# Cross-attention and expert layer on one core: order of the first two pairs' query tiles, one rotation moved to GpSimd, and the banks of two weight products

## The chip, the core and the metric

One core of a Trainium2 chip runs the kernel. The metric is the device time of one execution in microseconds (us). The program writes its own instruction streams, one for each engine: TensorE (PE), VectorE (DVE), ScalarE (ACT), GpSimd (POOL) and SyncE (SP, which only starts DMAs). An engine takes its instructions in the order written, and semaphores make it wait for another's.

## What is computed

The reference, cut to what matters. `x` is 2 x 256 rows of 256, `ctx` 2 x 512 rows of 64; there are 16 heads and 32 experts.

```
h = layernorm(x)
q = rope((h @ Wq.T per head) @ w_kc_q)          # 192 per head
scores = (q @ W_qr) @ (rope(ctx) @ W_kr).T      # 256 x 512 per head and batch
x = x + (softmax(scores) @ rope(ctx) @ w_kc_kv.T per head) @ Wo.T
h = layernorm(x)
top 4 of 32 experts by sigmoid(h @ gate.T) + bias, in 2 of 4 groups
x = x + sum of the chosen experts' swiglu(h) * weight + shared swiglu(h)
```

## The kernel before

**Tiling.** The 16 heads are worked in four groups of four, each group as two pairs. The attention consists of 64 score tiles (128 queries x 512 keys of one head and batch), numbered t. Pair 0 has tiles 0 to 7, pair 1 tiles 8 to 15, and so on. Three banks of PSUM (2, 3, 4) hold scores, two (5, 6) the transposed probabilities, bank 7 the attended sums, and banks 0 and 1 (`shared`) all that is prepared for later pairs. The change touches only the first 41 us of the program.

**Steps.** What is prepared is written as steps `(group, letter, index)`:

- `M0` to `M3`: the product of one head's two query weights (PE, L505); ACT casts it to the high part (L851, L852), DVE subtracts for the low part (L1054, semaphore `m_lo`).
- `A`, `B`, `C` with index j: the three 128-row tiles of pair j's queries, six matmuls each (L456 to L458). Tile A holds rows of the pair's first head, B of its second, C the rest of both.
- Rotation of such a tile. By GpSimd: ACT copies the tile out of its bank (L867) and half of it shifted (L868), DVE copies the other half shifted (L1061: the exchange, semaphore `q_swap`), then GpSimd does three operations (L361, L362, L364). By DVE straight from the bank (L1044 twice, L1046, L1047), when the tile stands in `AHEAD`; steps `x` and `z` name the place of the rotation of tiles A and C. The first B tile (`ALONE`) goes to GpSimd with all three copies by ACT (L864, L865, L868).
- `G`: product of the two rotation-side weights, into `gmat` (PE L511, ACT L856). `R0 R1 R2` (pair 0) and `P0 P1 P2` (pair 1): the rotated tiles A, B, C times `gmat`, added up in one bank (L537, L537, L540); then ACT casts (L875, L876) and DVE subtracts (L1080, L1082, semaphore `q_lo`), and the pair's scores can start.
- `N`: product of two output-side weights (PE L516, ACT L858). `K`: transposes of the keys (L554) with their high part (ACT L887) and low part (DVE L1093, semaphore `kT_lo`). `X`: transposes of the normalised rows. `W`: filler matmuls. `E`: a table load.

**A score tile.** PE computes it (L583, L584), DVE takes the row maximum (L1097), ACT the exponential with its sum (L893), PE transposes the probabilities (L595), ACT (t even) or DVE (t odd) copies them to `pT` (L902, L1115), and PE multiplies by the rows of ctx (L612, `attend`).

**What sets the order.** `PROLOGUE` is the list of steps ahead of the first score; `PLAN[g]` says which steps stand at which tile of group g. A step with "-" belongs to the group itself, one without it to the next group: `M0` in `PLAN[0]` is the second group's. `SEQ` joins them, and each engine walks the same list for its own share. `USED` are the steps of `SEQ` that take a bank. Those in `OWN_BANK` have a fixed one; the rest (`SHARED`) alternate between banks 0 and 1 in the order of the list, so that step n waits until step n-2 has left the bank: for an `M` that is `m_lo` of its subtraction, for `R` or `P` it is `q_lo`, for a tile in `AHEAD` its rotation, for anything else the copy out of the bank. An `R` or `P` counts at the place of its index 2, though its index 0 is the first to write. Scores of t wait for the exponential of t-3.

**Names of the change's place.** `first_turned` is the special form of the first query tile, `bank_free` the waits for a bank, `scores(0)` and `transposes(0)` the first of each. In the loop of PE `steps(0)` stands between scores 2 and scores 3; on ACT and DVE between the exponentials and maxima of tiles 2 and 3 and the work of tile 0's probabilities.

## Time and profile before

| | |
|---|---|
| median of 3 runs | 302.06 us (301.9 to 302.15) |
| the profiled execution | 301.82 us, of which the span of the profile is 299.5 us |
| TensorE busy | 282.5 us (94%), mean granted clock 0.995 |
| VectorE, ScalarE, GpSimd busy | 181.4, 156.4, 129.5 us |
| HBM | 30.38 MB read, 3.67 MB written |

Times of rows are us from the span's start. A timeline row gives the start, the time from the start of its first to the end of its last instruction, the engine, the line, the operation and its tiles, and in brackets the idle time before it with what ended that. Matmuls overlap: one of 512 columns in the fast format lasts 0.40 us in its row while the next starts 0.23 us after it. A plain f32 matmul has two records.

### The profile page before, as it was taken

To read this page: it belongs to the slowest core of one execution; us is meant where nothing else is said; L and a number is where in the kernel's file an instruction comes from. 1 tells how busy PE (TensorE), PEld (TensorE's weight loads), DVE (VectorE), ACT (ScalarE), POOL (GpSimd) and SP (SyncE) were. 2 spreads that over 40 slices of the span, in tenths; PEclk is the share of its full clock that TensorE was granted. 3 is DMA by queue.
4 is the path that set the end of the run, shared out by engine and by line. 5 is a ranking of instruction groups with operands and counts; after the bars stand their busy time and mean duration, and the time that the engine had idled before them with its cause. 6 is when DMAs were issued, how large, how long until landed. Compare 5 with 4: busy or idle time off the path is not lost.

```text
span 299.5 us, 5458 instructions
## 1 busy us (share of the span) xinstructions
PE 282.5 (94%) x1831; PEld 202.7 (68%) x1831; DVE 181.4 (61%) x434; ACT 156.4 (52%) x373; POOL 129.5 (43%) x121
## 2 busy tenths in 40 slices
PE   8988799999999999999999999978789999999982
PEld 6857568676777666787667777754567666676662
DVE  4877776576757777765854466158842233344676
ACT  2747469675785866777773355185212333343330
POOL 0656328791036770079940000000176555565572
PEclk9999999999999999999999999999999999999998
DMA  7962500001700001600039992402033544432234
GB/s 235 402 253 79 204 1 2 0 2 25 255 3 1 0 3 46 218 0 1 2 127 380 402 352 78 173 2 70 1 106 106 150 150 144 154 109 72 70 82 130
DMA packets 15994, 34.41 MB, mean 115 GB/s; under 512 B 2528, under 2 KB 8416, under 8 KB 15968
## 3 DMA queue, kind: packets, MB, share of 16 engines
q1 hardware_dynamic: 13664, 27.77, 26.0%
q0 software_dynamic: 2304, 6.29, 7.4%
q8 instruction: 16, 0.26, 0.4%
q14 instruction: 10, 0.08, 0.1%
HBM read 30.38 MB, written 3.67 MB: 114 GB/s over the span
## 4 chain that ended last, share of the span: by engine, by line
PE 85%; DVE 7%; DMA 2%; issue 2%; ACT 2%; POOL 1%; POOLq 0%; DVEq 0%; ACTq 0%
PE bank L719 10%; PE bank L612 10%; PE bank L595 9%; PE bank L583 5%; PE bank L562 5%; PE bank L584 4%; PE bank L740 4%; PE bank L456 4%; PE bank L458 4%; PE bank L457 4%; PE bank L505 3%; PE bank L708 3%; PE bank L537 3%; PE bank L685 3%; PE bank L540 3%; PE bank L463 2%
## 5 line engine op out<-in xcount | busy, mean ns | idle before, releaser
L1413 POOL DMA_INDIRECT rope<-xn_rows,idx x32 | 31.2, 974 | 83.3 <-DVE idx L1307 61.9
L893 ACT ACTIVATE prob<-bank,nmax 128x512 f32<-128x512 f32 x48 | 32.7, 685 | 38.9 <-DVE nmax L1097 38.9
L361 POOL TENSOR_TENSOR rtmp<-abuf,rope 128x512 f32<-128x512 f32 x20 | 25.7, 1284 | 60.4 <-PE bank L458 41.0
L1097 DVE TENSOR_REDUCE nmax<-bank 128x1 f32<-128x512 f32 x64 | 41.2, 685 | 8.7 <-PE bank L584 8.4
L719 PE MATMUL bank<-wall,nmat 128*64 (+1 forms) x256 | 31.2, 386 | 0.8 <-ACT nmat L968 0.8
L612 PE MATMUL bank<-pT,kvr 128*64 128x256 f32 x256 | 31.2, 386 | 0.0
L1115 DVE COPY pT<-bank 128x512 f32<-128x512 f32 x32 | 22.0, 687 | 13.1 <-PE bank L595 12.9
L583 PE MATMUL bank<-kdup,qsp 128*128 128x512 f32 x64 | 28.3, 442 | 1.2 <-ACT prob L893 1.2
L364 POOL TENSOR_TENSOR roped<-rtmp 128x512 f32<-128x512 f32 x20 | 25.9, 1295 | 1.6
L1314 DVE TENSOR_TENSOR kv<-bank,kv 128x256 f32<-128x256 f32 x16 | 6.8, 425 | 32.5 <-ACT kv L981 32.4
L595 PE MATMUL bank<-ident,prob 128*128 128x128 f32 x192 | 26.3, 273 | 0.0
L595 PEld LDWEIGHTS bank<-ident,prob 128*128 128x128 f32 x192 | 22.6, 141 | 4.9 <-issue 1.7
L362 POOL TENSOR_TENSOR rtmp<-abuf,rope 128x512 f32<-128x512 f32 x20 | 25.8, 1292 | 0.0
L584 PE MATMUL bank<-kdup,qsp 128*128 128x512 f32 x64 | 25.3, 395 | 0.0
L719 PEld LDWEIGHTS bank<-wall,nmat 128*64 128x64 f32 x256 | 16.9, 137 | 10.5 <-issue 3.5
L612 PEld LDWEIGHTS bank<-pT,kvr 128*64 128x64 f32 x256 | 16.9, 137 | 9.8 <-issue 2.8
L902 ACT COPY pT<-bank 128x512 f32<-128x512 f32 x32 | 18.9, 592 | 7.5 <-PE bank L595 7.2
L1061 DVE COPY abuf<-bank 64x512 f32<-64x512 f32 x20 | 13.7, 684 | 14.7 <-ACT abuf L867 14.4
L968 ACT COPY nmat<-bank 128x512 f32<-128x512 f32 x16 | 9.4, 585 | 23.3 <-PE bank L708 23.3
L1418 POOL DMA_INDIRECT ctT<-y_rows,place x16 | 16.3, 1017 | 10.3 <-PE bank L719 3.7
L456 PE MATMUL bank<-xnT,msplit 128*128 128x512 f32 x46 | 20.6, 447 | 0.0
L583 PEld LDWEIGHTS bank<-kdup,qsp 128*128 128x128 f32 x64 | 12.0, 188 | 9.2 <-issue 7.4
(217 smaller groups left out, 559.8 us busy)
## 6 DMA issues: line engine op xcount, KB each, us to landing
wall<-in_w_exp SPq DMA_DIRECT2D x32, 384.0 KB, 7.5
wring<-in_w_attn SPq DMA_DIRECT2D x16, 224.0 KB, 4.3
wring<-in_w_attn SPq DMA_DIRECT2D x4, 640.0 KB, 8.1
y_rows<-nmat SPq DMA_DIRECT2D x10, 256.0 KB, 2.1
wring<-in_w_attn SPq DMA_DIRECT2D x4, 512.0 KB, 7.0
rope<-in_rope_q SPq DMA_DIRECT2D x1, 768.0 KB, 7.0
x_sb<-in_x SPq DMA_DIRECT2D x1, 512.0 KB, 3.6
xn_rows<-xn SPq DMA_DIRECT2D x4, 128.0 KB, 1.7
```

Source lines behind the costliest of these rows:

```text
L361: eng.tensor_tensor(t0.rearrange("p (b s) -> p b s", b=B), own.rearrange("p (b s) -> p b s", b=B), cos, ALU.mult)
L362: link(eng.tensor_tensor(t1.rearrange("p (b s) -> p b s", b=B), other.rearrange("p (b s) -> p b s", b=B), sin, ALU.mult))
L364: return eng.tensor_tensor(roped[:, j, k, :], t0, t1, ALU.add)
L456: pe.matmul(out_ap, a_hi, b_hi, start=first, stop=False)
L583: pe.matmul(s_ps[t % 3][:, :], q, kdup[:, 0, b * L:(b + 1) * L], start=True, stop=False)
L584: pe.matmul(s_ps[t % 3][:, :], q, kdup[:, 1, b * L:(b + 1) * L], start=False, stop=True) \
L595: mm = pe.transpose(t_ps[t % 2][:, lc * P:(lc + 1) * P], probs[t % 4][:, lc * P:(lc + 1) * P], ident[:, :])
L612: mm = pe.matmul(pv_ps[hh * DC:(hh + 1) * DC, 0:S], kvr[:, b * LC + lc, 0, :], pT[:, (2 * n + hh) % PR, lc, :], start=(lc == 0), stop=(lc ...
L719: mm = pe.matmul(hu_ps[j % 2][s * BLK:(s + 1) * BLK, (u % 2) * 2 * I:(u % 2 + 1) * 2 * I], xTu[:, u % XS, dc, s * BLK:(s + 1) * BLK], wall ...
L893: act.activation(probs[t % 4], s_ps[t % 3][:, :], ACT.Exp, bias=nmax[:, t:t + 1], accum_out=psum_e[:, t:t + 1]).then_inc(s_exp, 1)
L1097: dve.tensor_reduce(nmax[:, t:t + 1], s_ps[t % 3][:, :], AX.X, ALU.max, negate=True).then_inc(s_max, 1)
L1413: pool.indirect_dma_start(xg[:, u % XG, :], None, xn_dram, bass.IndirectOffsetOnAxis(idx[:, u:u + 1], 0)) \
```

## The change

Six edits. (1) In `PROLOGUE` B of pair 0 comes ahead of A and takes the form `first_turned`; A follows. (2) The two N products get banks 2 and 3 and other places: N0 behind R0, N1 behind R2. (3) The last step of the prologue, B of pair 1, becomes `FIRST`; PE does it where it did, but ACT takes its copies behind the exponentials of tiles 0 and 1, and DVE its exchange behind their maxima. (4) C of pair 1 leaves `AHEAD`: its rotation goes from DVE to GpSimd, with two copies by ACT and an exchange by DVE. (5) On PE only G of pair 1 stays between scores 2 and 3; C of pair 1 stands behind scores 3. (6) At tile 4 the order is P0, P1, A0, P2 in place of P0, P1, P2, A0; A0 is the second group's first query tile.

```diff
--- before.py
+++ after.py
@@ -287,7 +287,7 @@
 
 
         PLAN = [
-            {0: "-G1", 1: "-C1 -z1", 2: "M0", 3: "M1", 4: "-P0 -P1 -P2 A0", 6: "B0", 7: "C0 G0", 8: "M2 M3", 9: "A1 G1", 10: "B1 R0 R1 R2", 11: "C1", 13: "N0", 15: "P0 P1 P2"},
+            {0: "-G1 -C1", 2: "M0", 3: "M1", 4: "-P0 -P1 A0 -P2", 6: "B0", 7: "C0 G0", 8: "M2 M3", 9: "A1 G1", 10: "B1 R0 R1 R2", 11: "C1", 13: "N0", 15: "P0 P1 P2"},
             {0: "-N1", 3: "M0 M1", 6: "A0 B0 M2", 7: "G0 M3 C0", 9: "z0 A1 B1", 10: "R0 R1 R2", 11: "C1", 12: "G1", 14: "P0 P1", 15: "P2 N0"},
             {1: "-N1", 2: "M0", 3: "M1", 6: "A0 B0", 7: "M2 C0", 8: "G0 M3", 10: "A1 B1", 11: "R0 R1 R2 C1", 13: "N0", 14: "G1", 15: "N1"},
             {0: "-P0 -P1 -P2", 2: "O0 O1 O2 O3", 8: "O4", 11: "S0", 15: "O5 O6"},
@@ -299,18 +299,19 @@
             for s in PLAN[g].get(t % TPG, "").split():
                 yield (g, s[1], int(s[2])) if s[0] == "-" else (g + 1, s[0], int(s[1]))
 
-        PROLOGUE = [(0, s[0], int(s[1])) for s in "W6 M0 M1 W1 X0 M2 E0 W1 A0 x0 B0 C0 z0 M3 G0 K0 N0 R0 N1 R1 R2 A1 B1".split()]
-
-        SEQ = PROLOGUE + [s for t in range(TILES) for s in steps(t)]
+        PROLOGUE = [(0, s[0], int(s[1])) for s in "W6 M0 M1 W1 X0 M2 E0 W1 B0 A0 x0 C0 z0 M3 G0 K0 R0 N0 R1 R2 N1 A1".split()]
+        FIRST = (0, "B", 1)
+
+        SEQ = PROLOGUE + [FIRST] + [s for t in range(TILES) for s in steps(t)]
         USED = [s for s in SEQ if s[1] in "MGABCN" or (s[1] in "RP" and s[2] == NQT - 1)]
         USE = {s: u for u, s in enumerate(USED)}
         BY_DVE = [(NPG * g + i, "xyz".index(kind)) for g, kind, i in SEQ if kind in "xyz"]
         BY_POOL = [(p, k) for p in range(NP) for k in range(NQT) if (p, k) not in BY_DVE]
 
-        AHEAD = ((0, "A", 0), (0, "C", 0), (0, "C", 1))
+        AHEAD = ((0, "A", 0), (0, "C", 0))
         ALONE = (0, "B", 0)
         TURNED = [s for s in USED if s[1] in "ABC" and s not in AHEAD and s != ALONE]
-        OWN_BANK = {(0, "M", 2): 2, (0, "M", 3): 3, (0, "C", 0): 4, (0, "B", 1): 5}
+        OWN_BANK = {(0, "M", 2): 2, (0, "M", 3): 3, (0, "C", 0): 4, (0, "N", 0): 2, (0, "N", 1): 3, (0, "B", 1): 5}
         SHARED = [s for s in USED if s not in OWN_BANK]
 
         def work(u):
@@ -464,7 +465,7 @@
 
             def first_turned(u):
 
-                m_hi, m_low = m_v[:, 0, :, 0, 0, :], m_v[:, 1, :, 0, 0, :]
+                m_hi, m_low = m_v[:, 0, :, 0, 1, :], m_v[:, 1, :, 0, 1, :]
                 pe.wait_ge(wk_out, out_count(use(0, "M", 1)))
                 for dc in range(ND):
                     pe.wait_ge(xT_hi, dc + 1)
@@ -480,8 +481,10 @@
             def bank_free(u):
 
                 n = SHARED.index(USED[u]) if USED[u] in SHARED else 0
-                if USED[u] == (0, "B", 1):
+                if USED[u] == FIRST:
                     pe.wait_ge(kT_lo, 2)
+                elif USED[u][:2] == (0, "N"):
+                    pe.wait_ge(m_lo, OWN_BANK[USED[u]] + 1)
                 if n >= 2:
                     g, kind, i = SHARED[n - 2]
                     if kind == "M":
@@ -518,7 +521,7 @@
                     mm.then_inc(wk_full, 1)
                 elif kind in "ABC":
                     k = "ABC".index(kind)
-                    if u == use(0, "A", 0):
+                    if u == use(0, "B", 0):
                         first_turned(u)
                         return
                     pe.wait_ge(m_lo, HG * g + 2 * i + 2)
@@ -577,6 +580,7 @@
                 if t == 0:
                     pe.wait_ge(kT_lo, 2)
                     pe.wait_ge(m_lo, HG)
+                    pe.wait_ge(wk_out, out_count(use(0, "N", 1)))
                 if t >= 3:
                     pe.wait_ge(s_exp, t - 2)
                 q = qsp[:, p % QR, hh, b * S + st * P:b * S + (st + 1) * P]
@@ -587,8 +591,8 @@
             def transposes(t):
                 pe.wait_ge(s_exp, t + 1)
                 if t == 0:
-                    pe.wait_ge(wk_out, out_count(use(0, "B", 1)))
-                    pe.wait_ge(q_swap, TURNED.index((0, "B", 1)) + 1)
+                    pe.wait_ge(wk_out, out_count(use(*FIRST)))
+                    pe.wait_ge(q_swap, TURNED.index(FIRST) + 1)
                 if t >= 2:
                     await_out(pe, t - 2)
                 for lc in range(LC):
@@ -618,23 +622,23 @@
             for s in PROLOGUE:
                 step(*s)
             pe.wait_ge(kT_lo, 2)
+            step(*FIRST)
             for t in range(LOOK):
                 scores(t)
+            between, *behind = steps(0)
             for t in range(TILES):
                 if t % 2 == 0:
                     for u in range(t + LOOK, min(t + LOOK + 2, TILES)):
                         if u == LOOK + 1:
-                            for s in steps(0):
-                                step(*s)
+                            step(*between)
                         scores(u)
                 n, late = divmod(t - ALAG, 4)
                 if late == 0 and n >= 0:
                     attend(n)
                 if late == 1 and n >= 0:
                     quotients(n)
-                if t >= 1:
-                    for s in steps(t):
-                        step(*s)
+                for s in steps(t) if t else behind:
+                    step(*s)
                 if t % 2 == 0:
                     transposes(t)
                     transposes(t + 1)
@@ -912,6 +916,7 @@
                 step(*s)
             for t in range(LOOK):
                 exps(t)
+            step(*FIRST)
             for t in range(TILES):
                 if t % 2 == 0:
                     for u in range(t + LOOK, min(t + LOOK + 2, TILES)):
@@ -1125,6 +1130,7 @@
                 step(*s)
             for t in range(LOOK):
                 row_max(t)
+            step(*FIRST)
             for t in range(TILES):
                 if t % 2 == 0:
                     for u in range(t + LOOK, min(t + LOOK + 2, TILES)):
```

Where the instructions stand, at three places. First PE in the prologue, around the three matmuls of R (`roped,gmat`) and the two of each N (`wring 64x256`), before:

```order
L516 MATMUL bank1<-wring 64x256 [waits d_wn0,wk_out]
L516 MATMUL bank1<-wring 64x256
L537 MATMUL bank1<-roped,gmat 64x512 [waits rope_a,wk_out]
L516 MATMUL bank0<-wring 64x256 [waits d_wn0,wk_out]
L516 MATMUL bank0<-wring 64x256
L537 MATMUL bank1<-roped,gmat 64x512 [waits rope_p]
L540 MATMUL bank1<-roped,gmat 128x512 [waits rope_a]
L456 MATMUL bank0<-xnT,msplit 128x512 [waits m_lo,wk_out]
```

and now:

```order
L540 MATMUL bank1<-roped,gmat 64x512 [waits rope_a,wk_out]
L519 MATMUL bank2<-wring 64x256 [waits d_wn0,m_lo]
L519 MATMUL bank2<-wring 64x256
L540 MATMUL bank1<-roped,gmat 64x512 [waits rope_p]
L543 MATMUL bank1<-roped,gmat 128x512 [waits rope_a]
L519 MATMUL bank3<-wring 64x256 [waits d_wn0,m_lo]
L519 MATMUL bank3<-wring 64x256
L457 MATMUL bank0<-xnT,msplit 128x512 [waits m_lo,wk_out]
```

R0 no longer stands behind N0 in the same bank, and N1 has moved behind R2. Second DVE, from the exchange of B of pair 1 (`abuf<-bank5`) to the second group's first two subtractions (`msplit`), before:

```order
L1061 COPY abuf<-bank5 64x512 [waits q_own]
L1097 TENSOR_REDUCE nmax<-bank2 128x1 [waits s_mm]
L1097 TENSOR_REDUCE nmax<-bank3 128x1 [waits s_mm]
L1097 TENSOR_REDUCE nmax<-bank4 128x1 [waits s_mm]
L1097 TENSOR_REDUCE nmax<-bank2 128x1 [waits s_mm]
L1115 COPY pT<-bank6 128x4x128 [waits t_mm]
L1044 TENSOR_TENSOR rtmp<-bank0,pT 64x512 [waits wk_full,d_turn]
L1044 TENSOR_TENSOR rtmp<-bank0,pT 64x512
L1046 TENSOR_TENSOR rtmp<-bank0,rope 128x512 [waits d_rope]
L1047 TENSOR_TENSOR roped<-rtmp 128x512 [waits chain_v]
L1097 TENSOR_REDUCE nmax<-bank3 128x1 [waits s_mm,rope_a]
```

and now:

```order
L1102 TENSOR_REDUCE nmax<-bank3 128x1 [waits s_mm]
L1066 COPY abuf<-bank5 64x512 [waits q_own]
L1102 TENSOR_REDUCE nmax<-bank4 128x1 [waits s_mm]
L1102 TENSOR_REDUCE nmax<-bank2 128x1 [waits s_mm]
L1066 COPY abuf<-bank0 64x512 [waits q_own]
L1120 COPY pT<-bank6 128x4x128 [waits t_mm]
L1102 TENSOR_REDUCE nmax<-bank3 128x1 [waits s_mm]
L1102 TENSOR_REDUCE nmax<-bank4 128x1 [waits s_mm]
```

The exchange of B (`bank5`) stands behind the second maximum and ahead of the third; an exchange for C (`bank0`) stands where no instruction of C stood, and the four of its rotation are gone. Third PE at tile 4, P0 and P1 (`64x512`), P2 and the second group's A0, before:

```order
L537 MATMUL bank1<-roped,gmat 64x512 [waits rope_p,wk_out,m_lo]
L537 MATMUL bank1<-roped,gmat 64x512 [waits rope_p]
L540 MATMUL bank1<-roped,gmat 128x512 [waits rope_a]
L456 MATMUL bank0<-xnT,msplit 128x512 [waits m_lo]
```

and now:

```order
L540 MATMUL bank0<-roped,gmat 64x512 [waits rope_p,wk_out,m_lo]
L540 MATMUL bank0<-roped,gmat 64x512 [waits rope_p]
L457 MATMUL bank1<-xnT,msplit 128x512 [waits m_lo]
...
L543 MATMUL bank0<-roped,gmat 128x512 [waits rope_p]
```

P0, P1 and P2 now write bank 0, which the second group's M1 used last, in place of bank 1, which its M0 used last; P2 stands behind the six matmuls of A0 and waits for GpSimd in place of DVE.

## Rows read from the trace of the kernel before

**Rows 1.** The page's busy times.

```profile
PE 282.5 (94%) x1831; PEld 202.7 (68%) x1831; DVE 181.4 (61%) x434; ACT 156.4 (52%) x373; POOL 129.5 (43%) x121
```

**Rows 2.** Waits of PE up to 66 us: us in total, times, longest.

```profile
PE bank L505 <- DVE roped L1047: 0.5, 1, 0.5
```

**Rows 3.** Windows: length, then busy us of PE, PEld, DVE, ACT, POOL, clock, DMA.

```profile
211.00:214.00 3.00, 1.33 (x18) 1.21 (x18) 2.42 (x11) 1.43 (x4) 0.00 (x0) 1.00 0.00 0
```

**Rows 4.** Timeline of PE, the prologue.

```profile
18.55 0.64 PE L537 MATMUL bank<-roped,gmat 128*64 128x512 f32 x1 [0.86 <-ACT nmat L858]
...
19.65 0.64 PE L537 MATMUL bank<-roped,gmat 128*64 128x512 f32 x1
```

**Rows 5.** The chain that ended last, in order of time: start, us.

```profile
20.72 1.06 PE bank L540 x2
```

**Rows 6.** Timeline of DVE, the prologue.

```profile
12.17 1.39 DVE L1044 TENSOR_TENSOR rtmp<-bank,pT 64x512 f32<-64x512 f32 x2 [0.23 <-PE bank L477]
...
15.28 1.39 DVE L1044 TENSOR_TENSOR rtmp<-bank,pT 64x512 f32<-64x512 f32 x2
...
18.50 0.62 DVE L1054 TENSOR_TENSOR msplit<-bank,msplit 128x256 fp32r<-128x256 f32 x2
```

**Rows 7.** Timeline of ACT, the prologue.

```profile
13.49 0.59 ACT L864 COPY abuf<-bank 128x512 f32<-128x512 f32 x1 [0.95 <-PE bank L458]
```

**Rows 8.** Timeline of POOL, 14 to 29 us.

```profile
14.09 0.61 POOL L1390 COPY kvr<-kvr 128x512 f32<-128x512 f32 x1
15.41 1.27 POOL L361 TENSOR_TENSOR rtmp<-abuf,rope 128x512 f32<-128x512 f32 x1 [0.71 <-ACT abuf L868]
...
18.00 1.60 POOL L364 TENSOR_TENSOR roped<-rtmp 128x512 f32<-128x512 f32 x1
24.70 1.30 POOL L361 TENSOR_TENSOR rtmp<-abuf,rope 128x512 f32<-128x512 f32 x1 [5.11 <-DVE abuf L1061]
...
27.30 1.28 POOL L364 TENSOR_TENSOR roped<-rtmp 128x512 f32<-128x512 f32 x1
28.67 1.29 POOL L361 TENSOR_TENSOR rtmp<-abuf,rope 128x512 f32<-128x512 f32 x1
```

**Rows 9.** Timeline of DVE, 25 to 38 us.

```profile
25.23 0.68 DVE L1061 COPY abuf<-bank 64x512 f32<-64x512 f32 x1 [0.70 <-ACT abuf L867]
25.95 1.89 DVE L1097 TENSOR_REDUCE nmax<-bank 128x1 f32<-128x512 f32 x3
...
30.68 1.39 DVE L1044 TENSOR_TENSOR rtmp<-bank,pT 64x512 f32<-64x512 f32 x2 [0.77 <-PE bank L458]
...
33.53 1.29 DVE L1097 TENSOR_REDUCE nmax<-bank 128x1 f32<-128x512 f32 x2
36.16 0.62 DVE L1054 TENSOR_TENSOR msplit<-bank,msplit 128x256 fp32r<-128x256 f32 x2 [1.34 <-ACT msplit L852]
...
37.30 0.61 DVE L1054 TENSOR_TENSOR msplit<-bank,msplit 128x256 fp32r<-128x256 f32 x2
```

**Rows 10.** Timeline of ACT, 26 to 36 us.

```profile
26.67 0.69 ACT L893 ACTIVATE prob<-bank,nmax 128x512 f32<-128x512 f32 x1 [0.87 <-DVE nmax L1097]
...
27.35 0.68 ACT L893 ACTIVATE prob<-bank,nmax 128x512 f32<-128x512 f32 x1
...
29.74 0.47 ACT L856 COPY gmat<-bank 128x384 f32<-128x384 f32 x1
30.10 0.60 ACT L902 COPY pT<-bank 128x512 f32<-128x512 f32 x1
34.25 0.69 ACT L893 ACTIVATE prob<-bank,nmax 128x512 f32<-128x512 f32 x1 [3.56 <-DVE nmax L1097]
```

**Rows 11.** Timeline of PE, 24 to 37 us.

```profile
24.65 0.40 PE L584 MATMUL bank<-kdup,qsp 128*128 128x512 f32 x1
...
27.59 0.48 PE L583 MATMUL bank<-kdup,qsp 128*128 128x512 f32 x1 [0.95 <-ACT prob L893]
...
36.84 1.08 PE L537 MATMUL bank<-roped,gmat 128*64 128x512 f32 x4 [0.95 <-DVE msplit L1054]
```

## The prediction

> **What bounds the kernel now.** The page comes first: PE is busy 94% of the span, every other engine 61% or less [rows 1]. So PE's own work sets the time wherever PE has no wait, and an edit that removes no PE work can only win by shortening PE's waits. The list of PE's waits, cut to the first 66 us, then says which there are, and the timeline of PE where each stands. Four of some size lie where this change can touch them. At 18.55, R0 waits 0.86 us for ACT's copy of N0 [rows 4]. At 27.59, scores 3 wait 0.95 for the second exponential [rows 11]. M1 of the second group waits 0.5 for DVE's rotation of C of pair 1 [rows 2].  At 36.84, P0 waits 0.95 for the subtraction of the second group's M0 [rows 11]. From there to the output products of the last group PE has no wait in that list. So the whole effect of this change is read from one point: how much earlier or later P0 starts than 36.84. Behind it the same matmuls follow in nearly the same order.
>
> **The prologue.** B of pair 0 is now the first product. DVE took up the first product at 12.17 [rows 6], ACT took up the second at 13.49, behind an idle time of 0.95, so it had been free from 12.54 [rows 7]. Now ACT starts its three copies at 12.55, 0.94 earlier. GpSimd's rotation began at 15.41 [rows 8]; it cannot win all of it, because GpSimd's own copy of the ctx rows (L1390) ends at 14.70 [rows 8], so I start it at 14.79, 0.62 earlier. It took 4.19, to 19.60 [rows 8], so it ends at 18.98 and R1 starts at 19.03 in place of 19.65 [rows 4]. DVE's rotation of A moves the other way: 1.32 later, from 12.17 to 13.49. It takes 3.11 (12.17 to 15.28) and the one of C 3.22 (15.28 to 18.50) [rows 6], so C is rotated at 19.82. R1 to R2 took 1.07 (19.65 to 20.72), R2 took 1.06 [rows 4, 5]. Now R2 starts at 20.10, so C is in time by 0.28, and ends at 21.16. R0's wait of 0.86 is gone, but it was no gain: with R0 at 17.04, PE waits for GpSimd in R1 all the same. N1 stood inside the wait and now stands behind R2, where it costs PE 0.43 to 0.58; I take 0.49. So A of pair 1 starts at 21.65 in place of 21.78: **a gain of 0.13**.
>
> Here two engines meet. DVE's two rotations took 3.11 and 3.22 beside GpSimd's work [rows 6], while the one of C of pair 1, with GpSimd idle at its end, took 2.85 (30.68 to 33.53) [rows 9]; and GpSimd's L364 took 1.60 at 18.00 against 1.28 at 27.30 [rows 8]. What meets is the last of DVE's four operations (L1047), the one that reads SBUF alone. The two of these now fall at about 15.6 and 18.7, other places of GpSimd's rotation; I leave the stretch as it was, one on each engine. The Trainium skill (SBUF — State Buffer, Terms) has it that the two engines lock one port pair for a whole instruction and that the loser fully blocks. The trace shows stretches of a third of a microsecond, less than a whole 1.28 us instruction. By that rule GpSimd could end about 0.5 us later, and the sum would come out near 302.9.
>
> **The maxima ahead of the exchange.** DVE's first maximum began at 25.95 because the exchange of B of pair 1 (25.23) stood ahead of it [rows 9]. Its scores were ready at 25.05 (24.65 + 0.40 [rows 11]), 25.08 at DVE. With the 0.13 it now starts at 24.95, 1.00 earlier; the first exponential, 0.72 behind it, goes from 26.67 [rows 10] to 25.67, and scores 3 from 27.59 [rows 11] to 26.59. That is the change's gain, and if nothing came back it would be 1.00 us at PE.
>
> **What comes back.** The B copy now stands on ACT behind the second exponential and the exchange on DVE behind the second maximum, with the third and fourth maxima queued behind it. Exponentials follow each other by 0.68 or 0.66, so the copy starts at 27.01 (0.59 long), the exchange at 27.64, and the third maximum at 28.35, while in the old order it stood at 27.2, the third of three from 25.95 [rows 9]. The fourth starts 0.63 later and the fourth exponential at 29.75 in place of 29.06 (0.68 ahead of 29.74 [rows 10]). Then ACT copies G (to 30.43, and 0.36 until the next, as 29.74 to 30.10), copies C (30.79), DVE exchanges C (31.42), copies the probabilities of tile 1 (32.13) and takes the fifth maximum at 32.84. Before it was 33.53, behind the 2.85 us of C's rotation. So of the 2.85 taken from DVE only 0.69 remains, since ACT reaches C's copy so late. The fifth exponential goes from 34.25 [rows 10] to 33.56. On PE in that time: C (six matmuls, 1.40) runs at 27.05, hidden; the transposes of tile 2 now wait for the copy of tile 0's probabilities, which ACT makes behind C's two copies (31.97 to 32.55, formerly 30.10), and run at 32.6; M1 and scores 6 and 7 are done at 35.1. PE then waits for P0.
>
> **The bank.** P0 started 2.59 behind the fifth exponential (34.25 to 36.84), 0.06 behind the end of M0's subtraction (36.16 + 0.62). In the new order of the list A0 counts ahead of P2, so P0 to P2 take bank 0, whose last user is M1, and P0 waits for M1's subtraction. That one stands behind the copy of tile 3's probabilities and ended at 37.91 (37.30 + 0.61) [rows 9], 3.66 behind the fifth exponential. So P0 starts at 33.56 + 3.66 + 0.06 = 37.28 in place of 36.84. **A loss of 0.44.** C's rotation on GpSimd covers itself: A's starts at about 24.6, one takes 3.97 (24.70 to 28.67 [rows 8]), B's runs from 28.6 to 32.5 and C's to 36.5; P2 at 39.7 is in time. Three GpSimd operations and two ACT copies (1.2 us) thus cost nothing further. P2 behind A0 delays pair 1's `q_lo` by what A0 takes, 1.40; by the same walk it is there 0.3 before scores 8 want it, since they move by 0.44 too.
>
> **The sum.** -0.13 (N and GpSimd) - 0.87 (exchange) + 0.31 (what comes back until the fifth exponential: 1.00 less 0.69) + 1.13 (bank: 3.72 for 2.59) = +0.44 us. The profiled execution took 301.82, so it would take 302.26; the median of the runs is 302.06, 0.24 above it, so the median goes to **302.5 us**, no change by the bound of 0.2% (0.60 us), which is about what a measurement can tell.
>
> **Rivals.**
>
> Slower: the first rotations are late. Start point: R1, if GpSimd's rotation ends after about 19.3. DVE's two additions each meet a GpSimd instruction; if GpSimd is stretched twice by the 0.32 seen once, and N1 costs its full 0.58, A of pair 1 starts near 22.1, 0.3 later than before, and all behind it shifts: 0.44 + 0.45 = +0.89, 302.95. For it: 1.60 against 1.28. Against it: of the three rotations that GpSimd made up to 33 us only one was stretched, and DVE's additions are short. It decides nothing as long as R1 starts before 19.2. The rule above is this mechanism at its strongest. Chance 0.20.
>
> Faster: the turn of the bank costs nothing. If P0 goes at M0's subtraction, or the pair of subtractions comes closer together, the 0.69 at the fifth exponential reaches PE: 36.15, and 301.4. For it: that is the gain the chain above carries up to 33.56. Against it: the written order and `bank_free` give P0 the wait for M1. Chance 0.12; with it go errors of the same sign, every link of the chain from 24.95 to 37.28 being a little shorter than taken.
>
> Nothing moves: the parts cancel to within 0.2 us, because ACT's copy of C comes earlier than I think or the slack of GpSimd and DVE, both ahead after this, removes small waits later. 302.1. Chance 0.11.
>
> The clock: PE would be idle from 35.1 to 37.3, longer than any wait of before. In the window from 211 to 214 us PE was busy 1.33 of 3 us, with one wait of 1.7, and the granted clock stayed 1.00, that is 2.4 GHz [rows 3]. If the clock fell to 1.2 GHz behind the new wait, the 3.4 us of matmuls up to the transposes of tile 4 would take twice as long: 305.9. The Trainium skill (TensorE: Matmul & The Clock Gate, What's actually happening) says that an idle array is throttled to 1.2 GHz; no row here shows a fall. Chance 0.02.
>
> **How the numbers follow.** My forecast has 0.55, with a range of its own from 302.2 to 302.8 (each of the some nineteen links is good to 0.02, the start of A of pair 1 to 0.2). With the four rivals that makes 1.00. The range from 301.4 to 303.1 takes in the slower case and the nearer half of the faster one, and leaves out some 0.15. Faster by over 0.2% (below 301.46): the faster rival and a rest, 0.13. Slower by over 0.2% (above 302.66): 0.19 of the late rotations' 0.20, the clock's 0.02 and a share of 0.05 of the forecast's own, 0.26. Within: 0.61.
>
> **What would show it.** After the change: R1 at 19.0, A of pair 1 at 21.65, first maximum at 24.95, scores 3 at 26.6; the third maximum not before 28.3, with the wait put down to the exchange or ACT's copy; the fifth exponential at 33.5; then PE's longest wait up to 66 us, some 2.2 us, ahead of P0 and behind the subtraction of M1. It is wrong if P0 starts before 36.8, if PE has a new wait at the transposes of tile 0 or at scores 8, or if the granted clock leaves 1.00 between 35 and 41 us. Then the change's gain or loss lies at that place and not at the bank.

## The result and the profile after

The changed kernel takes 303.47 us (median of 20 runs, 301.67 to 305.54), the kernel before, on the same chip, 302.2 (20 runs, 301.67 to 303.5). The ratio is **1.0039, 95% interval 1.0024 to 1.0053**: slower by some 1.2 us, where 302.5 and no change had been forecast. 303.47 lies outside the forecast's range of 301.4 to 303.1. The profiled execution took 304.0 us, its span 302.0 against 299.5.

The page's busy times and the granted clock in 40 slices, to be read against [rows 1]: PE's share is the same, GpSimd has the three operations of one more rotation. The single 7 of the clock lies in the routing (the choice of the experts), at 211 to 219 us, far behind the change.

```profile
PE 284.7 (94%) x1831; PEld 202.7 (67%) x1831; DVE 179.6 (59%) x431; ACT 157.7 (52%) x375; POOL 133.5 (44%) x124
...
PEclk9999999999999999999999999999799999999998
```

The waits of PE up to 66 us (in total, times, longest):

```profile
PE bank L540 <- POOL roped L365: 2.0, 1, 2.0
PE bank L540 <- DVE msplit L1059: 1.8, 1, 1.8
PE bank L464 <- DVE prob L1028: 1.5, 1, 1.5
PE bank L599 <- ACT pT L906: 0.9, 1, 0.9
PE bank L508 <- ACT gmat L860: 0.2, 1, 0.2
```

The two largest are at places that the prediction named, ahead of R1 and ahead of P0, though it had the one at P0 as the longest. The third lies ahead of the first products and is in the other kernels too. The fourth is the forecast wait of tile 2's transposes for the copy of tile 0's probabilities. The timeline of PE shows where they stand (R1, R2, N1, first and fourth scores, P0):

```profile
20.34 1.07 PE L540 MATMUL bank<-roped,gmat 128*64 128x512 f32 x2 [1.99 <-POOL roped L365]
21.34 1.12 PE L543 MATMUL bank<-roped,gmat 128*128 128x512 f32 x2
22.39 0.65 PE L519 MATMUL bank<-wring 128*64 128x256 f32 x4
...
25.88 0.40 PE L587 MATMUL bank<-kdup,qsp 128*128 128x512 f32 x1
...
28.20 0.48 PE L587 MATMUL bank<-kdup,qsp 128*128 128x512 f32 x1
...
38.77 1.08 PE L540 MATMUL bank<-roped,gmat 128*64 128x512 f32 x4 [1.79 <-DVE msplit L1059]
```

R1 was forecast at 19.03 and stands at 20.34; P0 was forecast at 37.28 and stands at 38.77, against 36.84 [rows 11]. GpSimd's timeline shows why R1 is late: its first work on ctx starts at 10.39, behind the load of its table, the last copy ends at 15.63, and two of the three operations of the rotation, of 1.77 and 1.60, are longer than the 1.27 of [rows 8].

```profile
10.39 0.74 POOL L1392 TENSOR_TENSOR kvr<-kv,kvtab 128x256 f32<-128x256 f32 x1 [9.95 <-DMA kvtab<-in_rope_kv]
...
15.02 0.61 POOL L1396 COPY kvr<-kvr 128x512 f32<-128x512 f32 x1
15.60 1.77 POOL L362 TENSOR_TENSOR rtmp<-abuf,rope 128x512 f32<-128x512 f32 x1
17.35 1.26 POOL L363 TENSOR_TENSOR rtmp<-abuf,rope 128x512 f32<-128x512 f32 x1
18.68 1.60 POOL L365 TENSOR_TENSOR roped<-rtmp 128x512 f32<-128x512 f32 x1
```

DVE's timeline answers to [rows 6, 9]: two additions beside that rotation (L1052), then first and second maximum, exchange of B, third and fourth maximum, exchange of C, fifth maximum, and the subtraction of M1.

```profile
15.55 0.69 DVE L1052 TENSOR_TENSOR roped<-rtmp 128x512 f32<-128x512 f32 x1
...
18.41 0.74 DVE L1052 TENSOR_TENSOR roped<-rtmp 128x512 f32<-128x512 f32 x1
...
26.55 1.29 DVE L1102 TENSOR_REDUCE nmax<-bank 128x1 f32<-128x512 f32 x2 [0.56 <-PE bank L588]
29.23 0.68 DVE L1066 COPY abuf<-bank 64x512 f32<-64x512 f32 x1 [1.40 <-ACT abuf L871]
29.95 1.29 DVE L1102 TENSOR_REDUCE nmax<-bank 128x1 f32<-128x512 f32 x2
33.01 0.68 DVE L1066 COPY abuf<-bank 64x512 f32<-64x512 f32 x1 [1.78 <-ACT abuf L871]
...
34.34 1.28 DVE L1102 TENSOR_REDUCE nmax<-bank 128x1 f32<-128x512 f32 x2
...
38.10 0.61 DVE L1059 TENSOR_TENSOR msplit<-bank,msplit 128x256 fp32r<-128x256 f32 x2
```

From the first maximum on all stands 1.5 to 1.6 us behind the forecast, and the distances are nearly those forecast: first to third maximum 3.40 (forecast 28.35 - 24.95 = 3.40), third to fifth 4.39 (forecast 32.84 - 28.35 = 4.49).

### The profile page after: what moved, and what is told of

Read it like the earlier page. It is cut to its first block, busy times and chain, and to the rows that moved or that the text cites. A ratio compares the mean times of both kernels' runs of the same rounds, so it can differ in the third digit from the quotient of the medians.

```text
span 302.0 us, 5459 instructions
## 1 busy us (share of the span) xinstructions
PE 284.7 (94%) x1831; PEld 202.7 (67%) x1831; DVE 179.6 (59%) x431; ACT 157.7 (52%) x375; POOL 133.5 (44%) x124
## 4 chain that ended last, share of the span: by engine, by line
PE 80%; DVE 5%; POOL 5%; DMA 3%; ACT 3%; issue 2%; SPq 1%; DVEq 0%; POOLq 0%; ACTq 0%
PE bank L616 10%; PE bank L723 9%; PE bank L599 9%; PE bank L587 5%; PE bank L744 5%; PE bank L565 5%; PE bank L588 4%; PE bank L689 3%; PE bank L457 3%; PE bank L459 3%; PE bank L458 3%; PE bank L540 3%; PE bank L712 3%; PE bank L543 3%; PE bank L508 2%
## 5 line engine op out<-in xcount | busy, mean ns | idle before, releaser
L362 POOL TENSOR_TENSOR rtmp<-abuf,rope 128x512 f32<-128x512 f32 x21 | 27.4, 1303 | 57.4 <-PE bank L459 41.3
L365 POOL TENSOR_TENSOR roped<-rtmp 128x512 f32<-128x512 f32 x21 | 27.2, 1294 | 1.6
L363 POOL TENSOR_TENSOR rtmp<-abuf,rope 128x512 f32<-128x512 f32 x21 | 26.9, 1282 | 0.0
L1066 DVE COPY abuf<-bank 64x512 f32<-64x512 f32 x21 | 14.4, 684 | 19.7 <-ACT abuf L871 19.6
L457 PE MATMUL bank<-xnT,msplit 128*128 128x512 f32 x46 | 19.9, 432 | 0.0
L459 PE MATMUL bank<-xnT,msplit 128*128 128x512 f32 x46 | 18.2, 396 | 0.0
```

Source lines behind the costliest of these rows:

```text
L362: eng.tensor_tensor(t0.rearrange("p (b s) -> p b s", b=B), own.rearrange("p (b s) -> p b s", b=B), cos, ALU.mult)
L365: return eng.tensor_tensor(roped[:, j, k, :], t0, t1, ALU.add)
L457: pe.matmul(out_ap, a_hi, b_hi, start=first, stop=False)
L459: return pe.matmul(out_ap, a_lo, b_hi, start=False, stop=last)
```

## The experiments

Every profile is read at three marks of PE's timeline: R1, the first score matmul (scores 0), and P0. The table gives the two distances between them, which say how the order of the work acts, and R1 itself, which says when GpSimd was done. The median of the kernel before differed by about 1 us from one set of measurements to another (301.96 to 303.18; 302.06 and 303.17 in two sets on one and the same chip), so a ratio is always against the kernel before, measured on the same chip in the same set, and times of different sets are not compared. A dash means a single execution. The kernels whose names end in look, look2 and look3 are repeated: before_look and after_look are the two kernels themselves, a_first_look, look2 and look3 are a_first.

| kernel | ratio to before (interval) | R1 | R1 to scores 0 | scores 0 to P0 | P0 |
|---|---|---|---|---|---|
| before | 1 | 19.65 | 4.76 | 12.43 | 36.84 |
| before_look | - | 19.32 | 4.75 | 12.44 | 36.51 |
| the change | 1.0039 (1.0024, 1.0053) | 20.34 | 5.54 | 12.89 | 38.77 |
| after_look | - | 18.96 | 5.54 | 12.88 | 37.38 |
| p2_first | 0.9977 (0.9964, 0.9990) | 18.88 | 5.55 | 11.74 | 36.17 |
| a_first | 1.0066 (1.0041, 1.0091) | 18.89 | 5.54 | 12.87 | 37.30 |
| a_first_look | - | 20.58 | 5.53 | 12.89 | 39.00 |
| look2 / look3 | - | 19.41 / 19.06 | 5.55 / 5.54 | 12.89 / 12.88 | 37.85 / 37.48 |
| a_first_p2_n | 0.9972 (0.9951, 0.9992) | 20.11 | 4.74 | 11.75 | 36.60 |
| max_only | 1.0028 (1.0016, 1.0041) | 19.57 | 4.76 | 12.92 | 37.25 |
| c_dve | 1.0046 (1.0030, 1.0062) | 19.54 | 5.54 | 12.92 | 38.00 |
| fill_p0 | 1.0031 (1.0016, 1.0046) | 19.16 | 5.53 | 12.89 | 37.58 |
| kv_early | 1.0031 (1.0005, 1.0058) | 17.89 | 6.26 | 12.89 | 37.04 |
| kv_early_p2 | 0.9973 (0.9959, 0.9987) | 18.77 | 6.27 | 11.76 | 36.80 |
| kv_late | 1.0028 (1.0015, 1.0042) | 19.55 | 5.54 | 12.88 | 37.97 |
| n_wait | 0.9995 (0.9981, 1.0010) | 20.39 | 4.75 | 12.88 | 38.02 |
| n_wait_p2 | 0.9960 (0.9944, 0.9975) | 20.01 | 4.76 | 11.75 | 36.52 |

**The turn of the bank, p2_first.** The list of the first group has P2 ahead of A0, as before:

```diff
-            {0: "-G1 -C1", 2: "M0", 3: "M1", 4: "-P0 -P1 A0 -P2", 6: "B0", ...
+            {0: "-G1 -C1", 2: "M0", 3: "M1", 4: "-P0 -P1 -P2 A0", 6: "B0", ...
```

> The changed kernel with P2 ahead of A0 at tile 4, so that P0 to P2 take bank 1 again and wait only for the second group's M0. Bank theory: P0 starts some 14.6 us behind the start of pair 1's A tile, against 15.7 in the changed kernel (38.77 - 23.05), the wait in front of P0 shrinks from 1.8 to about 0.7, and the whole is 1.1 us shorter than the changed kernel, about 0.1 above the kernel before. Rival (the loss is all in the prologue, and GpSimd's rotation of C, which ended at 37.93 in the changed kernel, would hold P2 anyway): PE's wait moves from P0 to P2 and the time stays within 0.3 us of the changed kernel's.

From the first scores to P0 it is 11.74 in place of 12.89: the turn costs 1.15, where 1.13 had been taken, and the wait ahead of P0 falls from 1.8 to

```profile
PE bank L540 <- DVE msplit L1059: 0.7, 1, 0.7
```

The time is 301.59 (12 runs, 300.93 to 301.99) beside 301.96: **this version beats both kernels**, where 0.1 above the kernel before had been expected. The ratio falls by 0.0062, some 1.9 us (1.3 to 2.5), more than the turn alone. No run stands out upward, while four of 20 of the change do (305.09 to 305.54).

**Which product comes first, a_first.** A0 is ahead of B0 again and is the one that `first_turned` makes, with all else of the change:

```diff
-PROLOGUE = ... "W6 M0 M1 W1 X0 M2 E0 W1 B0 A0 x0 C0 z0 M3 G0 K0 R0 N0 R1 R2 N1 A1"
+PROLOGUE = ... "W6 M0 M1 W1 X0 M2 E0 W1 A0 x0 B0 C0 z0 M3 G0 K0 R0 N0 R1 R2 N1 A1"
```

> The changed kernel with A of pair 0 made first, as before; all else stays. GpSimd theory (R1 waits for GpSimd's rotation of B, which has lost its spare time against the landing of the key table): GpSimd starts at 15.4, held by ACT's copies and not by its own work on the ctx rows, R1 starts at 19.65 and pair 1's A tile at 22.3 in place of 23.05; the time is 0.5 to 0.8 below the changed kernel's and its spread over the rounds is smaller. Rival (the late landing only shifts everything alike, whichever tile is first): A tile at 23.0, no difference.

The expectation missed: 304.13 (11 runs, 301.85 to 305.58), no better than the change, and its spread is larger. Putting the first two products back does not win back the loss. Its distances equal those of the change. Three more executions of this kernel (a_first_look, look2, look3) were to show what differs between executions of one program.

> The same kernel as a_first, one more look, since 8 of its 11 runs had a mean clock of 0.986 to 0.988 and took 303.2 to 305.6. If this run is one of those, the clock theory expects a stretch at half clock between 35 and 45 us beside the one at 210 to 216 us, costing 1.5 to 3.5 us in the matmuls P0 to the transposes of tile 4 and those behind; the rival expects no half clock there and an A tile of pair 1 later than 22.

> The same kernel as a_first, a second look. Of its 12 runs so far 5 took 304.3 us or more with a mean clock of 0.986 to 0.988, a pair of values that p2_first (12 runs, at most 302.0) and fill_p0 (12 runs, at most 304.0) do not show. Clock theory: a run of 304.3 or more shows a stretch at 1.2 GHz between 34 and 46 us, behind PE's wait ahead of P0. Rival: such a run shows full clock there, and the time is lost in the first 23 us or behind 190.

> The same kernel as a_first, a third look, with the same two expectations as the second: a stretch at 1.2 GHz between 34 and 46 us if the run takes 304.3 us or more by the clock theory, full clock there by the rival.

The first of them had a late load (GpSimd starts at 10.52, R1 20.58, P0 39.0) and took 304.19; look2, with full clock behind P0, took 303.74. look3 took 305.41 though its P0 is earlier than in look2. The windows of look3 (length, busy us of PE, PEld, DVE, ACT, POOL, clock, DMA) show why:

```profile
36.00:38.00 2.00, 0.52 (x4) 0.20 (x4) 2.00 (x7) 0.57 (x3) 0.65 (x1) 1.00 0.00 0
38.00:40.00 2.00, 2.00 (x9) 1.23 (x6) 1.00 (x4) 1.45 (x4) 0.00 (x0) 0.77 0.01 4
40.00:42.00 2.00, 2.00 (x5) 1.11 (x4) 0.40 (x1) 0.99 (x2) 0.00 (x0) 0.50 0.00 0
42.00:44.00 2.00, 2.00 (x15) 1.23 (x15) 0.99 (x3) 1.46 (x4) 1.48 (x2) 0.88 0.00 0
```

PE had been busy 0.52 of the 2 us from 36 to 38, and 1.6 us behind P0's start the granted clock fell to 0.50, that is 1.2 GHz, for some 3 us. Timeline of PE in look3 (P0, two matmuls of A0, the transposes of tile 4):

```profile
37.48 1.08 PE L540 MATMUL bank<-roped,gmat 128*64 128x512 f32 x4 [1.79 <-DVE msplit L1059]
...
38.83 0.41 PE L458 MATMUL bank<-xnT,msplit 128*128 128x512 f32 x1
39.06 0.61 PE L459 MATMUL bank<-xnT,msplit 128*128 128x512 f32 x1
...
42.45 1.06 PE L599 MATMUL bank<-ident,prob 128*128 128x128 f32 x8
```

and in look2:

```profile
37.85 1.08 PE L540 MATMUL bank<-roped,gmat 128*64 128x512 f32 x4 [1.79 <-DVE msplit L1059]
...
41.23 1.04 PE L599 MATMUL bank<-ident,prob 128*128 128x128 f32 x8
```

From P0 to the transposes it is 4.97 against 3.38: the fall costs **1.6 us**. That is the forecast's rival of the clock, seen in one of four profiles of this program, and in one of the nine profiles of all kernels that have a wait of some 1.8 us ahead of P0. look2 had been busy only 0.21 of the 2 us from 36 to 38, and its clock stayed at 1.00. The Trainium skill (TensorE: Matmul & The Clock Gate, What's actually happening) says that an idle array is throttled to 1.2 GHz; the trace agrees in part: the level is that, but it fell in one profile of nine, and while PE worked again.

**Filling the wait, fill_p0.** Six matmuls without use, into bank 7, stand ahead of P0:

```diff
                     u = use(g, kind, 2)
+                    if (g, kind, i) == (0, "P", 0):
+                        for _ in range(6):
+                            pe.matmul(pv_ps[:, :], kdup[:, 0, 0:P], kdup[:, 0, 0:L], start=True, stop=True)
```

> The changed kernel with six filler matmuls of 512 columns (0.23 us each, 1.4 us in all) on PE between scores 7 and P0, in the 1.8 to 2.2 us in which PE waits for M1's subtraction; they write bank 7, which nobody reads yet. Clock theory: the runs of 303 us and more of the changed kernel are those in which the granted clock fell behind the idle stretch ahead of P0 (mean clock 0.986 to 0.988 in the slowest); with the stretch filled the wait itself stays, P0 starts where it did, but no run lies above 303.5, the median is 302.0 to 302.5 and the mean clock is 0.991 or more. Rival (the spread comes from when the first loads land, or from GpSimd's rotation): median and spread as in the changed kernel, 303.4 with runs above 305.

The filler took 1.5 us, the wait fell from 1.8 to 0.4, and P0 stands where it stood (12.89). The expectation of the clock missed: the median, 303.22, is 1.16 above its kernel before (302.06), as the change's is above its own, so a fall behind this wait does not make the median. No run of 12 is above 303.98, where the change has four of 20 from 305.09 to 305.54 and kv_early three of 12 from 304.65 up. That the filler takes these highest runs away is not shown, since n_wait, which has the unfilled wait of 1.8, had no high run in 12 either. Nor does a run's mean granted clock tell whether it had such a fall: before_look has 0.984 with a fall in the routing alone, and look3, with both, 0.986.

**The load ahead of GpSimd, kv_early, kv_early_p2, kv_late.** ctx and its table are loaded ahead of the last query weight (kv_early; kv_early_p2 the same on p2_first), or behind the sine table (kv_late).

```diff
-            for i in range(1, HG):
+            for i in range(1, HG - 1):
                 load_group(0, f"m{i}")
+            sp.dma_start(kv[:, :, :], ctx_kv).then_inc(d_kv, 16)
+            sp.dma_start(kvtab[:, :, :, :], rope_kv).then_inc(d_kv, 16)
+            load_group(0, f"m{HG - 1}")
```

> The changed kernel with the loads of ctx and its rotation table issued ahead of the fourth head's weights instead of behind them, 224 KB sooner in the queue. GpSimd theory: GpSimd starts on the ctx rows 0.5 us sooner than it would, and R1, pair 1's A tile and the end all follow by about that, 0.5 us below the changed kernel; GpSimd's first rotation starts right behind its own work in either case. Rival (ACT's copies hold the rotation, or the loss is elsewhere): no difference within the spread.

> The changed kernel with P2 ahead of A0 and with the loads of ctx and its table ahead of the fourth head's weights: the two repairs together. If both theories hold: GpSimd starts on the ctx rows at 8.4, pair 1's A tile at 21.3, P0 at 35.9, PE's wait ahead of P0 is 0.7, no run above 302.5, and the median is 0.3 below p2_first's 301.6, 0.7 to 0.9 below the kernel before. Rival (the landing plays no part in the time): as p2_first, 0.4 below the kernel before.

> The changed kernel with the load of DVE's sine table (256 KB) ahead of those of ctx and its table. Landing theory: GpSimd starts 0.5 later on the ctx rows than in the changed kernel, nothing of GpSimd's time is spare, and R1, pair 1's A tile, P0 and the end follow by the whole 0.5. Rival (GpSimd's rotation is not what R1 waits for in most runs): no difference from the changed kernel's 303.5.

GpSimd started at 8.36 and 8.08, and R1 went to 17.89 and 18.77; but then DVE's rotation of C was late for R2, and R1 to the first scores grew from 5.54 to 6.26:

```profile
PE bank L544 <- DVE roped L1053: 0.7, 1, 0.7
```

So the wait moves to DVE: kv_early's ratio, 1.0031, cannot be told from the change's 1.0039, and kv_early_p2 (0.9973) is no better than p2_first (0.9977). kv_late, meant to make R1 later still, started at 9.96, inside the spread that all have, so it says nothing of what a later load costs. It shows another thing: DVE's addition started 0.04 behind GpSimd's first multiplication and took 1.78 in place of 0.69, and GpSimd's next operation 1.71. First GpSimd's timeline, then DVE's:

```profile
15.20 1.27 POOL L362 TENSOR_TENSOR rtmp<-abuf,rope 128x512 f32<-128x512 f32 x1
16.43 1.71 POOL L363 TENSOR_TENSOR rtmp<-abuf,rope 128x512 f32<-128x512 f32 x1
...
15.24 1.78 DVE L1052 TENSOR_TENSOR roped<-rtmp 128x512 f32<-128x512 f32 x1
```

**The maxima alone, max_only.** The kernel before, with B of pair 1 taken out of the prologue to a place of its own, so that its exchange stands behind the first two maxima:

```diff
-... K0 N0 R0 N1 R1 R2 A1 B1".split()]
+... K0 N0 R0 N1 R1 R2 A1".split()]
+        FIRST = (0, "B", 1)
```

> The kernel before with only the exchange of B of pair 1 moved behind the maxima and exponentials of tiles 0 and 1. The walk of the changed kernel, applied here: scores 3 start 0.9 earlier (26.7), the third maximum 1.2 later, but the fifth maximum still stands behind DVE's rotation of C, which starts at about 30.7 as before, so P0 stays within 0.2 of 36.84 and the time within 0.3 of the kernel before. Rival (the earlier maxima are worth what they gain at scores 3): 0.9 us faster.

Scores 3 came 0.95 earlier (26.64 for 27.59), as walked. But P0 is later by 0.41, where at most 0.2 had been expected, the time is 0.85 above the kernel before (1.0028), where at most 0.3 had been, and a new wait stands ahead of the transposes of tile 0, for the exchange:

```profile
PE bank L596 <- DVE abuf L1064: 1.2, 1, 1.2
```

In the change the product C of pair 1 stands ahead of those transposes and fills that time. **c_dve** takes it away from there again: p2_first with C's product behind the transposes and its rotation by DVE (`{0: "-G1", 1: "-C1 -z1", ...}` and `(0, "C", 1)` in `AHEAD`).

> The kernel p2_first with C of pair 1 rotated by DVE out of its bank again and made behind the transposes of tiles 0 and 1, as before the change. By the walk the fifth maximum moves from about 32.4 back to about 33.4, because C's product comes some 1.6 us later on PE and DVE's rotation takes 2.85 in place of a copy of 0.7: P0 about 0.6 later than in p2_first (36.8 against 36.2) and the time about 0.5 above it. Rival (GpSimd's rotation of C is worth nothing, and p2_first gains only by the order of the matmuls of R and N): no difference from p2_first.

The same wait of 1.2 is back and P0 stands 12.92 behind the first scores, 1.18 more than in p2_first, about twice the 0.6 expected; the ratio, of six runs only, is higher by 0.0069, some 2 us for the 0.5 expected. What the edit of the maxima gains is thus lost at once unless work of PE is moved along with it; how much of the 1.18 is the place of C and how much its engine this run does not part.

**The place of N1, a_first_p2_n, n_wait, n_wait_p2.** a_first_p2_n has A first, P2 ahead of A0 and N1 between R0 and R1. n_wait moves N1 alone, to the place between R0 and R1 and to a bank where it waits for no subtraction; n_wait_p2 does it on p2_first. The edit of n_wait:

```diff
-PROLOGUE = ... "W6 M0 M1 W1 X0 M2 E0 W1 B0 A0 x0 C0 z0 M3 G0 K0 R0 N0 R1 R2 N1 A1"
+PROLOGUE = ... "W6 M0 M1 W1 X0 M2 E0 W1 B0 A0 x0 C0 z0 M3 G0 K0 R0 N0 N1 R1 R2 A1"
-        OWN_BANK = {(0, "M", 2): 2, (0, "M", 3): 3, (0, "C", 0): 4, (0, "N", 0): 2, (0, "N", 1): 3, (0, "B", 1): 5}
+        OWN_BANK = {(0, "M", 2): 2, (0, "M", 3): 3, (0, "C", 0): 4, (0, "N", 0): 2, (0, "N", 1): 7, (0, "B", 1): 5}
-                elif USED[u][:2] == (0, "N"):
+                elif USED[u] == (0, "N", 0):
-                    pe.wait_ge(wk_out, out_count(use(0, "N", 1)))
+                    pe.wait_ge(wk_out, out_count(use(0, "N", 0)))
```

> The changed kernel with A of pair 0 first, N1 back between R0 and R1 (in bank 3), and P2 ahead of A0: of the change remain the maxima ahead of the exchange, C's rotation on GpSimd and the banks of N. If the two losses are the prologue and the bank, and they add: pair 1's A tile starts at 21.8, P0 at 36.4, and the time is 0.45 us below the kernel before (ratio 0.9985). Rival (C's rotation on GpSimd or the late exchange costs by itself): P0 at 36.8 or later, no gain.

> The changed kernel with the second output-side product N1 back inside a wait of PE (directly ahead of R1) and in bank 7, so that it waits for no subtraction and the first scores do not wait for it. Theory (the step of the prologue was mis-sized: N1 behind R2 costs PE 0.78 us, not 0.49, and the bank turn 0.46): from R2 to the first scores 3.76 instead of 4.54, from there to P0 12.9 as in every kernel of this bank order; the median 0.7 to 0.9 below the changed kernel, that is about 302.7 beside a kernel before at 302.2, ratio about 1.001. If the lateness is a matter of the landing and the clock alone, with N1 worth the 0.49 of the prediction or less, the median falls by 0.5 at most, and runs above 305 stay.

> The same edit on the version with P2 ahead of A0. Both theories: 11.75 from the first scores to P0. Mis-sized N1: 0.8 below the version with P2 first alone (ratio 0.9977 to before), so ratio about 0.995, some 300.7 beside a kernel before at 302.2, and no run above 303. If N1 is worth 0.3 to 0.5, ratio 0.9962 to 0.9968. If GpSimd's rotation ends so early that PE is not waiting ahead of R1, the gain is smaller by what N1 then delays R1.

In n_wait GpSimd is as late as in the profile of the change, so the two can be laid side by side: N1 runs inside the wait, and A of pair 1 follows R2 at once.

```profile
17.73 1.03 PE L519 MATMUL bank<-wring 128*64 128x256 f32 x6
20.39 1.07 PE L540 MATMUL bank<-roped,gmat 128*64 128x512 f32 x2 [1.63 <-POOL roped L365]
21.39 1.13 PE L543 MATMUL bank<-roped,gmat 128*128 128x512 f32 x2
21.95 0.80 PE L457 MATMUL bank<-xnT,msplit 128*128 128x512 f32 x1
```

R1 to the first scores is 4.75 for 5.54: **N1 behind R2 costs 0.79 us, not 0.49**. The ratio falls from 1.0039 to 0.9995, by 1.3 us with an interval of some 0.6 to each side. n_wait_p2 has 0.9960, the lowest of all (301.84, 12 runs, beside 303.17). That lies between the 0.995 expected if N1 is worth 0.8 and the 0.9962 expected if it is worth 0.5, so this ratio alone does not decide between the sizes, and its interval overlaps that of p2_first; the distance of 4.76 decides. a_first_p2_n, without the two losses but with A first, has P0 at 36.60 and 0.9972, for 36.4 and 0.9985 expected.

**The two kernels once more, after_look and before_look.**

> The changed kernel once more. Theory of the landing: R2 to the first scores 4.54 and from there to P0 12.89 again, whatever the start; GpSimd starts its ctx copies anywhere from 8.3 to 10.5, and R2 follows it, so that R2 lies between 19.6 and 21.6. If instead the change itself makes GpSimd late, the ctx copies start after 10.2 again and R2 is at 21.3.

> The kernel before once more. Theory: R2 to the first scores 3.76 and from there to P0 12.43 again; since GpSimd's rotation waits for ACT's copies, R2 stays within 0.2 of 20.65 unless the landing is later than 10.2. If before follows the landing as closely as the changed kernel, R2 moves with the start of the ctx copies.

On one chip: 303.75 and 303.11 us. Here GpSimd started at 9.34 and R1 stood at 18.96, 0.07 before the forecast; P0 at 37.38, 0.10 behind it. So the late start in the profile of the change belongs to that execution. Even in this early one the rotation took 4.38 (14.58 to 18.96), for the 4.19 of [rows 8]:

```profile
14.58 1.26 POOL L362 TENSOR_TENSOR rtmp<-abuf,rope 128x512 f32<-128x512 f32 x1
15.81 1.74 POOL L363 TENSOR_TENSOR rtmp<-abuf,rope 128x512 f32<-128x512 f32 x1
17.63 1.27 POOL L365 TENSOR_TENSOR roped<-rtmp 128x512 f32<-128x512 f32 x1
```

before_look kept 4.75 and 12.44, but not R2 to within the 0.2 expected: R1 and R2 stand 0.33 earlier, though its load landed as in the profile of before (GpSimd's first operation 9.48 for 9.45). There the rotation (15.08) follows GpSimd's own copy directly, and that copy took 0.95 for the 0.61 of [rows 8]. So before has slack there in some executions, not in all.

It also had a fall of the clock to 0.50 at 210 to 216 us, in the routing. Such falls stand in 15 of the 18 profiles, of either order, and belong to no edit. What one costs depends on where it comes. From the sixteen matmuls of `xnT` to the ten of `kdup` it is 4.19 us in before (212.82 to 217.01), without a fall. Timeline of PE in before_look, then in the change:

```profile
212.49 1.89 PE L805 MATMUL bank<-xnT 128*64 128x64 f32 x16 [0.56 <-DVE xnT L1242]
...
218.22 2.65 PE L663 MATMUL bank<-kdup 128*128 128x512 f32 x10
```

```profile
214.82 1.09 PE L809 MATMUL bank<-xnT 128*64 128x64 f32 x16
...
219.02 2.63 PE L667 MATMUL bank<-kdup 128*128 128x512 f32 x10
...
222.34 0.44 PE L712 MATMUL bank<-ident,rope 128*128 128x128 f32 x2 [0.47 <-DMA rope<-xn_rows,idx]
```

In before_look, where the clock was still down in that stretch, it is 5.73; in the change, where it had fallen earlier (0.53 from 211 to 214), 4.20: that fall cost nothing. So the span behind P0 runs from 262.6 to 264.7 us over the profiles without look3, in kernels of either order, and a single profiled time says little of an edit.

## Why the prediction was wrong

**The step that failed is the prologue's:** "a gain of 0.13", A of pair 1 starting at 21.65 in place of 21.78. It had two terms, and both were mis-sized.

- *N1 costs 0.49.* It costs 0.79 (n_wait against the change), beyond the 0.58 given as its upper bound. The prediction shows no working for its 0.43 to 0.58. Alone behind R2, N1's four matmuls take 0.65 in their row (22.39), and A's first matmul, which in n_wait starts beside R2 (21.95, 0.80 long), loses that overlap. This term is shown.
- *GpSimd's rotation starts 0.62 earlier.* That number rested on one execution, in which the ctx copies ended at 14.70 and the rotation waited 0.71 for ACT. The load of GpSimd's table lands at another time in each execution: its first operation stood anywhere from 9.02 to 10.52, without the two kernels that load early. With A first the rotation waited for ACT in three of eight profiles (0.71, 0.80, 1.25) and followed the ctx copies directly in the other five; with B first it followed them in all eight. So in most executions with A first there was no such wait to win back.

How much was won? Over the eight profiles with B first (the change, after_look, n_wait, n_wait_p2, p2_first, fill_p0, c_dve, kv_late) R1 stands at 19.60 on average, over the eight with A first and the old loads at 19.57: nothing won. But the load happened to land later in those with B first (GpSimd's first operation at 9.88 on average, for 9.48), though of their edits only that of kv_late touches the loads. Counted from that operation, R1 stands 9.72 behind it with B first and 10.09 with A first. So of the 0.62 some 0.37 is left at an equal landing. This is an estimate from sixteen profiles, and no run fixed the landing.

In five of the eight with B first R1 stands 9.57 to 9.62 behind that operation, as forecast (19.03 - 9.45 = 9.58), by two small errors that cancel: the rotation follows the copies at once, some 0.1 sooner than taken, and lasts some 0.1 longer. In the other three (the change, n_wait, n_wait_p2), those with the latest landings, it is 9.91 to 9.98: there both of DVE's additions met an operation of GpSimd. The forecast had left one stretch on each engine. In the change both fell on GpSimd (1.77 and 1.60), and DVE had C rotated at 19.15 (18.41 + 0.74) in place of 19.82.

**The sizes that held.** R1 to P0 was to be 18.25 (19.03 to 37.28). It is 18.43, 0.30 of N1 too long and 0.11 too short behind the first scores. There 13.00 had been walked over maxima, exchange, copies and bank, and 12.89 measured. The bank's 1.13 is 1.15. The maxima's gain is there, scores 3 only 2.32 behind the first scores (25.88 to 28.20) where it was 3.18 before (24.41 to 27.59), and is given back as said. The wait ahead of P0 is behind M1's subtraction as forecast; its length was 1.8 for "some 2.2".

**The sum with the measured terms:** +0.44 forecast, +0.30 for N1, +0.25 for what is missing of the 0.62, -0.11: about +0.9 us. The ratio says 1.18 us, with an interval of 0.7 to 1.6, and fill_p0 and kv_late, whose distances are the same, have 0.94 and 0.85 by theirs. The sum lies within the interval; whether the last 0.3 us has a cause of its own is open. In the profiled execution P0 is 1.93 behind before's because the landing was 0.94 later as well (10.39 for 9.45). The 0.5 us more of span behind P0 in that profile is a wait of 0.47 for a load of gathered rows at 222.34, behind the routing, which the profile of before does not have.

**The rivals.** "The first rotations are late" is in part what happened. Its start point, R1 at 19.3, was passed in five of the eight profiles with B first. In three of them both additions met GpSimd, as the rival has it, and the landing was late too; in c_dve and kv_late, with R1 at 19.54 and 19.55, only the landing was (9.96). The forecast took a load's landing as fixed and two meetings of DVE and GpSimd as one. In all 18 profiles that rotation had one operation of GpSimd lengthened by 0.3 to 0.5 us, or two. The Trainium skill (SBUF — State Buffer, Terms) says that of two such instructions the loser is blocked for the whole of the other's. These rows agree to within 0.14 us: in the change L362 began 0.05 behind an addition that ended at 16.24, and took 1.77, ending at 17.37, where 16.24 and its own 1.27 make 17.51; in kv_late the addition, begun 0.04 behind a multiplication that ended at 16.47, ended at 17.02, where 16.47 and its own 0.69 make 17.16. The forecast by that rule, near 302.9, was the nearer one in number, but of the miss accounted for above the larger term is N1, which it does not touch. "The turn is free" is out: 1.15. "Nothing moves" is out. "The clock" happens: in one of the nine profiles with such a wait, priced at 3.4 us and worth 1.6, since it comes late and holds for some 3 us only. A chance of 0.02 was too little for a wait longer than any before. It may explain the highest runs and not the median.

**Open.** Why a_first has more high runs (five of 11 from 304.37 up) than the change (four of 20) or n_wait (none of 12), with the same wait ahead of P0, was not settled. Nor was the difference of 0.0062 between the change and p2_first parted fully: the turn accounts for 1.15 of some 1.9 us.

## What to carry to other kernels

A gain that consists of starting an engine earlier counts only up to what else that engine waits for, and a load's landing in one profile is one draw. Take it from several executions, and compare kernels at an equal landing, before making it a number. A step that is moved loses the overlaps it had, and so does its new neighbour: price it at its new place. Where an order is written by hand, see which bank each product falls on: one name moved in a list cost 1.15 us, and undoing it gave the faster kernel.

## What was not expected of the hardware

The granted clock fell with PE busy, 1.6 us behind the end of a 1.79 us wait, and in one of four profiles of the same program; the wait alone does not decide it. A fall in the routing cost 1.5 us in before_look and nothing in the change, by where it came. The same loads, in the same order, let GpSimd start at 9.02 to 10.52 in different executions (both ends of that range in executions of a_first). And an operation of 0.69 us on DVE took from 0.69 to 1.78 us by when it began against GpSimd's.
